# Earlier halved loads of context and key weights, keys ahead of transposes and values, in a cross-attention and expert-FFN kernel

## The reference

```
hs = layernorm(x);  at = nan_clean(ctx)            # NaN -> 0, +-inf -> +-10000
q, k, v = heads(hs @ Wq.T + bq), heads(at @ Wk.T + bk), heads(at @ Wv.T + bv)     # 16 heads of 32
probs = softmax(where(mask, clip(q k^T / sqrt(32), -50, 50), -50))
delta = clip(rs, 0, 0.3) * (probs v @ Wo.T + bo)
x = x + layernorm(delta) * gamma + beta
y = layernorm(x);  gate = top 2 of 8 of softmax(y @ router.T)
x = x + sum_e gate_e * (silu(y @ down_e.T) @ up_e)                                # 8 experts, 16 wide
```

## Time and profile before

| | |
|---|---|
| runs of the kernel | 203.36 us median of 3 (202.25, 203.36, 205.74) |
| span of the profiled execution, first to last instruction | 200.5 us |
| time of that execution around its span | not recorded; the median lies 2.86 us above the span |
| busy TensorE / VectorE / ScalarE / GpSimd | 95% / 70% / 53% / 45% of the span |
| chain that ended last | 87% TensorE, 3% VectorE, 2% ScalarE, 2% DMA, 1% GpSimd, 3% issue |
| granted TensorE clock, mean | 0.980 of full speed |

### The profile page before, as it was taken

One profiled execution on the slowest core, in us unless ns is written; L12 is line 12 of the kernel. 1 busy time (PEld: TensorE's weight loads), 2 busy tenths in 40 slices (PEclk: granted clock), 3 DMA queues, 4 the chain that ended last, 5 costly groups with the idle time before them and its releaser, 6 DMA issues.

```text
span 200.5 us, 3747 instructions
## 1 busy us (share of the span) xinstructions
PE 189.9 (95%) x1342; PEld 143.3 (71%) x1342; DVE 141.2 (70%) x320; ACT 105.7 (53%) x216; POOL 91.1 (45%) x152
## 2 busy tenths in 40 slices
PE   7899999969899999999999999999999999999593
PEld 7798846637466886758787866887876688888372
DVE  1989958989361863956438755886758797869884
ACT  2386271465596446182777566776354572365500
POOL 5610087930989677050446676062232871433200
PEclk9999999999999999999999999999999999999858
...
GB/s 204 357 331 363 366 22 68 144 3 84 134 124 107 58 63 0 0 29 92 17 104 0 0 119 3 0 0 6 117 3 98 20 194 125 2 0 105 52 105 262
DMA packets 12045, 19.45 MB, mean 97 GB/s; under 512 B 2267, under 2 KB 4315, under 8 KB 12028
## 3 DMA queue, kind: packets, MB, share of 16 engines
...
## 4 chain that ended last, share of the span: by engine, by line
PE 87%; DVE 3%; issue 3%; ACT 2%; DMA 2%; POOL 1%; ACTq 0%; POOLq 0%; DVEq 0%
PE ps_r L380 60%; PE ps_t L404 8%; PE ps_v L518 5%; PE ps_v L477 4%; PE ps_r L450 4%; PE ps_v L464 4%; DMA xs<-x 2%; PE ps_v L521 1%; ACT stage L718 1%; PE ps_v L517 1%; DVE xs L1105 1%; DVE ln_st L978 1%; DVE xs L1053 1%; PE ps_r L542 1%; PE ps_v L380 0%
## 5 line engine op out<-in xcount | busy, mean ns | idle before, releaser
L1387 POOL TENSOR_TENSOR attt_lo<-wk,attt_hi 128x512 fp32r<-128x512 f32 x16 | 21.6, 1368 | 18.2 <-ACT attt_hi L727 18.2
L380 PE MATMUL ps_r<-hst_hi,wq_hi 128*128 128x512 f32 x64 | 26.6, 415 | 0.4 <-ACT stage L718 0.4
L380 PE MATMUL ps_r<-hst_hi,wq_lo 128*128 128x512 f32 x64 | 25.3, 395 | 0.0
L380 PE MATMUL ps_r<-wo_hi,attt_lo 128*128 128x512 f32 x64 | 25.2, 394 | 0.0
L380 PE MATMUL ps_r<-wo_hi,attt_hi 128*128 128x512 f32 x64 | 25.2, 394 | 0.0
L380 PE MATMUL ps_r<-wo_lo,attt_hi 128*128 128x512 f32 x64 | 25.2, 394 | 0.0
L380 PE MATMUL ps_r<-hst_lo,wq_hi 128*128 128x512 f32 x64 | 25.2, 394 | 0.0
L1383 POOL TENSOR_TENSOR xs<-xs,beta_bc 128x512 f32<-128x512 f32 x16 | 21.0, 1334 | 3.6 <-ACT hs L700 3.6
L706 ACT ACTIVATE q_sb<-ps_r,bq_sb 128x512 f32<-128x512 f32 x16 | 11.0, 689 | 21.9 <-PE ps_r L380 21.9
L988 DVE TENSOR_TENSOR hst_lo<-ps_t,hst_hi 128x512 fp32r<-128x512 f32 x16 | 10.6, 686 | 12.1 <-ACT hst_hi L686 12.1
L1036 DVE TENSOR_TENSOR wk<-ps_v,wk 128x512 f32<-128x512 f32 x16 | 10.4, 685 | 11.0 <-PE ps_v L477 11.0
...
## 6 DMA issues: line engine op xcount, KB each, us to landing
...
xs<-x SPq DMA_DIRECT2D x3, 1024.0 KB, 5.5
...
wk<-wk_t SPq DMA_DIRECT2D x1, 1024.0 KB, 8.2
stage<-wq_t SPq DMA_DIRECT2D x1, 1024.0 KB, 10.4
xs<-wv_t SPq DMA_DIRECT2D x1, 1024.0 KB, 10.2
xs<-wo_t SPq DMA_DIRECT2D x1, 1024.0 KB, 8.2
```

The lines of the kernel that those rows point to most:

```text
L380: last = pe.matmul(dst, w, m, start=start and i == 0, stop=stop and i == n - 1)
L1387: pool.tensor_tensor(attt_lo[:, :, c, :], att[:, c, :].rearrange("p (t n) -> p t n", t=NT), attt_hi[:, :, c, :].bitcast(F32), ALU.subtract ...
```

## The change

The context and `wk` are loaded in halves of two chunks each, alternating, ahead of x, each half with its own semaphore; `wv` comes ahead of `wq`; the six small loads are issued by ScalarE; `bv` comes first behind the cleaning, then x of batch 1 (which therefore waits for the cleaning now). VectorE cleans the context first and takes the statistics after it; the finite mark of each half is made by GpSimd (`finite_marks`). TensorE computes both halves of the keys, then transposes, with the values between them, in the two banks of `RING_V` rather than in `RING_R`; the second set of filler products is gone and the first has 15 in place of 22; the expert means come after the fourth query. ScalarE's and VectorE's lists are moved to suit.

The diff, with the list edits already shown, the new semaphores and unchanged lines cut:

```diff
-WARM = 22
-WARM_MORE = 5
+WARM = 15
...
-    "K0 K1 K2 K3 Q00 Q01 V0 V1 Q02 Q03 S00 S01 S02 S03 S04 S05 S06 S07 Q10 Q11 S10 S11 S12 S13 Q12 Q13 "
+    "K0 K1 K2 K3 Q00 Q01 Q02 Q03 S00 S01 S02 S03 S04 S05 S06 S07 Q10 Q11 S10 S11 S12 S13 Q12 Q13 "
...
-    "m0 s00 s01 v00 v01 v02 v03 s10 v10 v11 s11 v12 v13 s20 f00 f01 f02 s21 v20 v21 v22 v23 f03 f10 f11 "
+    "V0 V1 m0 s00 s01 v00 v01 v02 v03 s10 v10 v11 s11 v12 v13 s20 f00 f01 f02 s21 v20 v21 v22 v23 f03 f10 f11 "
...
+            sp.dma_start(ctx_sb[:, 0:2, :], wide(ctx_t)[:, 0:2, :]).then_inc(ctx_in, 16)
+            sp.dma_start(wk[:, 0:2, :], wide(wk_t)[:, 0:2, :]).then_inc(wk_in, 16)
+            sp.dma_start(ctx_sb[:, 2:KC, :], wide(ctx_t)[:, 2:KC, :]).then_inc(ctxb_in, 16)
+            sp.dma_start(wk[:, 2:KC, :], wide(wk_t)[:, 2:KC, :]).then_inc(wkb_in, 16)
             sp.dma_start(xs[:, 0:2, :], x_tiles[:, 0:2, :]).then_inc(x0_in, 16)
             sp.dma_start(xs[:, 2:NT, :], x_tiles[:, 2:NT, :]).then_inc(x0b_in, 16)
-            sp.dma_start(ctx_sb[:, :, :], wide(ctx_t)).then_inc(ctx_in, 16)
-            sp.dma_start(wk[:, :, :], wide(wk_t)).then_inc(wk_in, 16)
+            sp.dma_start(wv_raw[:, :, :], wide(wv_t)).then_inc(wv_in, 16)
             sp.dma_start(wq_raw[:, :, :], wide(wq_t)).then_inc(wq_in, 16)
...
+            sp.wait_ge(ctx_ok, 2)
+            sp.dma_start(bv_bc[:, :], rows(bv, P)).then_inc(bv_in, 16)
             sp.dma_start(xs[:, NT:2 * NT, :], x_tiles[:, NT:2 * NT, :]).then_inc(x1_in, 16)
-            sp.wait_ge(ctx_ok, 2)
...
                 if b == 2:
-                    sp.wait_ge(mm_full, ring_r.count("V1", every=True))
+                    sp.wait_ge(v_full, ring_v.count("V1"))
...
             def values(j):
-                k = take(f"V{j}")
+                k = take_one(ring_v, f"V{j}", v_free)
...
+            act.dma_start(bk_sb[:, :], bk).then_inc(bqk_in, 16)
+            act.dma_start(bq_sb[:, :], bq).then_inc(bqk_in, 16)
+            for half in range(2):
+                act.dma_start(mask_sb[half * T:(half + 1) * T, :], mask_t).then_inc(mask_in, 16)
+            act.dma_start(rs_raw[:, :], rs.broadcast_to([P, 1])).then_inc(rs_bo_in, 16)
+            act.dma_start(bo_raw[:, :], rows(bo, 33)).then_inc(rs_bo_in, 16)
             for t in range(NT):
                 hs_norm(0, t)
...
             def clean_take(half):
-                cs, n = slice(2 * half, 2 * half + 2), 4 * half
+                cs, n = slice(2 * half, 2 * half + 2), 3 * half
+                dve.wait_ge(ctx_part, n + 2)
+                dve.copy_predicated(ctx_clean[:, cs, :], ctx_notnan[:, cs, :], ctx_lim[:, cs, :]).then_inc(ctx_part, 1)
                 dve.wait_ge(ctx_part, n + 3)
-                dve.copy_predicated(ctx_clean[:, cs, :], ctx_notnan[:, cs, :], ctx_lim[:, cs, :]).then_inc(ctx_part, 1)
-                dve.wait_ge(ctx_part, n + 4)
+                dve.wait_ge(finite_ok, half + 1)
                 dve.copy_predicated(ctx_clean[:, cs, :], ctx_finite[:, cs, :], ctx_sb[:, cs, :]).then_inc(ctx_ok, 1)
...
+            dve.wait_ge(ctx_in, 16)
+            dve.wait_ge(zeroed, 1)
+            clean(0)
+            dve.wait_ge(ctxb_in, 16)
+            clean(1)
             dve.wait_ge(x0_in, 16)
             ln_stats(range(2))
             dve.wait_ge(x0b_in, 16)
             ln_stats(range(2, NT))
...
+            def finite_marks(half):
...
+                pool.wait_ge((ctx_in, ctxb_in)[half], 16)
+                pool.tensor_scalar(ctx_finite[:, cs, :], ctx_sb[:, cs, :], 0.0, 0.0, ALU.mult, ALU.is_equal
+                                   ).then_inc(finite_ok, 1)
...
             pool.memset(average[:, :], 1.0 / H).then_inc(average_ok, 1)
             pool.memset(ctx_clean[:, :, :], 0.0).then_inc(zeroed, 1)
+            finite_marks(0)
+            finite_marks(1)
```

More of the change, by code:

```diff
@@ L472, in weigh @@
                 if b == 0:
[L473 removed]
+                    pe.wait_ge(v_free, ring_v.count("V1"))
                 for i in range(4):
@@ L537, in _ @@
                 pe.matmul(ps_r[3][:, 0:P], average[:, :], average[:, :], start=True, stop=True)
+            pe.wait_ge(wk_in, 16)
+            pe.wait_ge(ctx_ok, 1)
+            keys(0)
+            pe.wait_ge(wkb_in, 16)
+            pe.wait_ge(ctx_ok, 2)
+            keys(1)
             pe.wait_ge(ident_ok, 1)
@@ L540, in _ @@
             hs_transpose(0, 1)
-            for _ in range(WARM_MORE):
-                pe.matmul(ps_r[3][:, 0:P], average[:, :], average[:, :], start=True, stop=True)
-            pe.wait_ge(wk_in, 16)
-            pe.wait_ge(ctx_ok, 1)
-            keys(0)
+            values(0)
             hs_transpose(0, 2)
             hs_transpose(0, 3)
-            pe.wait_ge(ctx_ok, 2)
-            keys(1)
+            values(1)
             pe.wait_ge(wq_hi_ok, KC)
@@ L790, in _ @@
             hs_hi(0, 1)
+            act.wait_ge(bqk_in, 32)
+            for m in range(KC):
+                key_out(m)
+            hs_hi(0, 2)
+            hs_hi(0, 3)
             act.wait_ge(wq_in, 16)
@@ L793, in _ @@
                 act.copy(wq_hi[:, c, :], wq_raw[:, c, :]).then_inc(wq_hi_ok, 1)
-            hs_hi(0, 2)
-            hs_hi(0, 3)
-            act.wait_ge(bqk_in, 32)
-            for m in range(KC):
-                key_out(m)
             query_out(0, 0)
@@ L807, in _ @@
             hs_norm(1, 3)
-            experts_high()
             query_out(0, 2)
             query_out(0, 3)
+            experts_high()
             hs_hi(1, 0)
```

45 lines of the change are left out of this document (14 added, 31 removed).

## The result

The changed kernel is slower: a median of 207.9 us over four runs (206.19, 207.63, 208.17, 208.62) against 203.26 us for the kernel before, ratio **1.0253 (1.0209 to 1.0298)**. The profiled execution is the quickest of the four, 206.19 us with a span of 204.3 (before 200.5). Busy shares are 93% for TensorE, 70% for VectorE, 51% for ScalarE, 47% for GpSimd.

A forecast was written before the change was run, and what follows sets the result against it. TensorE was taken to bound the kernel nearly to the end, with query(1, 0) started 1.8 us later by VectorE's chain: span 200.5 + 1.8 = 202.3, with 2.86 above the span 205.2 us, range 201.8 to 207.8.

The forecast's parts named there:

- The loads: Start of the kernel: 2.95 us per MiB, x at 8.8 and 10.3, 0 to 0.95 later for small loads, taken as nothing.
- The cleaning: First on VectorE: 2.4 us a half without the mark, 1.0 in all for stretching by two marks, context clean at 9.5.
- the bounds of 0.43 to 1.33: Finite mark on GpSimd: between 0.43 us (the same on VectorE) and 1.33 (GpSimd's beta additions, same size, two inputs).
- The full lock of the rival: VectorE and GpSimd share a port lock; two marks at full length add 1.7 us at the context: 206.9; chance 0.08.
- The statistics: VectorE, four tiles of x behind the cleaning: 2.85 us from 9.5, ending at 12.35.
- the chain: From x's statistics through wq_hi and first query (23.2), batch 1's statistics (33.35), to scores at 39.75, 1.0 later than before.
- hst_lo(1, 0): VectorE, batch 1: reached at 41.25 to 42.3, which is 1.5 to 2.6 late; 1.8 taken, moving query(1, 0) as much.
- The offset: Added to the predicted span: 2.86 us, by which the earlier kernel's median of 203.36 lay above its profiled span.
- TensorE as the bound: Rival: VectorE's chain is shorter, scores start between 36.5 and 38.7, up to 2.2 us earlier, 201.2 to 203.3; chance 0.20.
- The clock's rival: TensorE's clock falls in the hole before scores(0, 0); costs 1 to 4 us, taken at 2.4: 207.6; chance 0.22.
- what would refute it: Sign against the forecast in the new profile: a granted TensorE clock near 0.5 between 36 and 50 us.
- Expert means later: only centre_experts and experts_high wait: Expert means behind the fourth query: cost nothing more, as both waiting steps were already counted.

## Why the prediction was wrong

The forecast was 205.2 us and within 2%; 207.9 lies just above its range and is slower. The mechanism held: VectorE is the later one, and query(1, 0) carries its lateness to the end. The step that failed is the pace of the loads, and with it the start of VectorE's chain. Of the 2.7 us by which the time was missed, 2.0 are in the span (204.3 against 202.3) and 0.7 in what lies above it.

- **The loads, the failing step.** The forecast worked by bytes at the pace of whole loads and took the six small loads at nothing. The first half of ctx came at 3.83 (3.7 worked out), but the second at 7.64 (5.85) and x at 11.06 (8.8, at most 9.75). Between 3 and 10 us 283 GB/s moved, against 371 before. With the small loads back on SyncE's queue it was 335, and x came 1.1 us earlier; with whole loads besides, 362. Moving the small loads to ScalarE's queue, which was to be hidden, was thus the larger part in these profiles, the halves the smaller one.
- **The cleaning** was right by luck. A mark took 2.17 us, outside the bounds of 0.43 to 1.33: the beta addition was no upper bound for another operation with another output type. But a half took 3.07 and 3.05 us, against 2.9 in the sum (2.4 and half a microsecond for the mark). The mark stretched VectorE's tensor_tensor from 0.69 to 1.10, and the last predicated copy waited for it; the two copies kept their 0.73 and 0.74. The full lock of the rival is not what happened. That the context was clean at 10.69 instead of 9.5 is the second half's late landing in the main.
- **The statistics** waited for x, not for the cleaning (0.38 us ahead of 11.06), and started at 11.06 instead of 9.5: 1.56 late. From there on **the chain was right** link by link, within 0.2 us: wq_hi at 21.43 (20.0 + 1.4), first query 24.89 (23.2 + 1.7), end of batch 1's statistics 34.98 (33.35 + 1.6), scores 41.26 (39.75 + 1.5). One link has another cause than the forecast's: ScalarE's own order did not set the time of the last two hst_hi ahead of wq_hi. They waited for transposes that stand behind the first half of the values on TensorE, which the forecast took to fit in without cost:

```profile
20.47 1.07 ACT L680 CAST hst_hi<-ps_t 128x512 fp32r<-128x512 f32 x2 [0.58 <-PE ps_t L399]
```

- **hst_lo(1, 0)** was taken 1.8 late and came 3.75 late: 1.6 from the start, and 0.3 in the list from batch 1's statistics on (8.50 us against 8.18), in which gamma took 1.56 and was expected to be stretched less.
- **From there to query(1, 0)** the forecast had no change; it took 6.32 us instead of 5.74. With the filler products, at the full clock, it took 5.82 (43.44 to 49.26), although the clips were as long there (1.79 and 1.15, amid GpSimd's additions, which now fall there). So this is the clock's price here, 0.5 us, which is gone again at the weighted values, where VectorE holds. Together 1.8 + 1.6 + 0.3 + 0.6 give 4.3 of the 4.33 late, of which 0.5 is made up by the end.
- **The offset.** The sum was the span plus 2.86. The profiled execution has 1.89 around its span, 206.19 in all; the other three are 1.4 to 2.4 us above it, with spans of 205.7 to 206.4. Two of them had a lower mean clock (0.967 and 0.964 against 0.975), the third did not; what else they do differently no profile here shows.

Of the rivals, TensorE as the bound is out (it waited 1.99 and 1.03 us). The clock's rival came true in its sign, 0.50 at 42 to 46, which the prediction had named as what would refute it, but not in its price, 1 to 4 us: in the profiled execution most of the time it took lay in waits for VectorE, and the 0.5 that was left at query(1, 0) was gone at the weighted values; it cost 1.26 at query(1, 0) when those waits were gone. "Expert means later: only centre_experts and experts_high wait" was right for this kernel and wrong as a statement on the means: they were a second bound 1.3 us behind the first (there at about 37.2, when VectorE came at 38.55), and cost 2.64 us once the first was moved.

What the forecast had in hand and did not use is that the change opens a wait on the engine that decides, just ahead of its full stretch (5.85 us as measured), with 3.9 us of work behind it that needed nothing but loads.
